# Adding h2 to the node update by an identity product in PSUM instead of an add on VectorE

## The chip, the cores and the metric

One core of a Trainium2 chip runs the whole kernel as one program. The metric is the device time of one execution in microseconds (us). The kernel before took 8569.4 us as the median of three runs (8554.72, 8569.40 and 8579.12).

## What is computed

A stack of four graph layers over 50,000 nodes with 128 features and 25,000 edges: two attention convolutions, three hops of LightGCN, a message-passing layer, and three GCN convolutions. Each layer is entered through a layer norm and relu, and added to its input. The part that the change touches is the third layer's update with what surrounds it:

```
h = max(layernorm(x), 0)                                  # h2
upd = relu([h, aggregated] @ Wu1 + bu1) @ Wu2 + bu2
y = h + upd
out2 = (y - mean(y)) * rsqrt(var(y) + eps) * gamma + beta
x = x + out2                                              # x3
h = max(layernorm(x), 0)                                  # h3
x0 = relu(h @ fc1 + fc1_b); three convolutions; x = x + (... @ fc2 + fc2_b)
```

Most nodes receive no edge, so for them `aggregated` is zero and the convolutions need no neighbours. The kernel computes every node row as if it were such a row, in dense groups, and rows with edges are computed again in later phases that overwrite them.

## The kernel before

The phase `light_and_tail` (`phase_light_and_tail`, class `Tail`) runs two things side by side.

The **tail** does the dense work on all node rows: 98 groups of 4 x 128 rows, each group a tile of 128 partitions x 512 values. It is a software pipeline of 105 steps. In step n, group n is loaded and its first statistics are taken, group n-1 gets h2 and its transpose, group n-2 gets the update and y, group n-3 gets the normed y and x3, group n-4 gets h3 and fc1, and groups n-5 to n-7 go through the convolutions and the output. Every engine has its own function for a step (`vector_step`, `scalar_step`, `tensor_step`, `sync_step`), and inside a step each engine executes its items in the order in which they are written; engines meet only through semaphores. `after(engine, signal, m, k)` makes group m wait until group m-k has given the signal; it is how buffers come free.

The order inside step n that matters here:
- **TensorE**: the update of group n-2 into the PSUM bank `psY` (a bf16 product with ones that brings in the bias bu2, then four products of 128x128 with Wu2); the first convolution of n-5 (`conv_lone`, into `psC1`); the transposes of h2 of n-1 (`psT`); the last convolution of n-6 (`conv2`, into `psU`); the transposes of h3 of n-4; `Wu1a` of n-1; the second convolution of n-5 (`conv1`, into `psC2`); `fc1` of n-4 (`psF`); the output of n-6 (`psO`). A float32 product appears in the trace as two matmuls.
- **ScalarE**: `uT` of n-2 (after Wu1a); `x0T` of n-5 (after fc1 of the step before); h2 of n-1 (four activations on 128x128); `yn` of n-3 (four); a root; `h2T`; `x3T` of n-6 (after conv2); h3 of n-4 (four); two roots; `h3T`.
- **VectorE**: statistics of x of group n; sums of the hops (all but the last of this step); `g2T`; the output add; the addition of beta to x, and the product of `yn` with gamma (both n-3); `g1T` of n-5 (reads `psC1`); x3 of n-3; y of n-2, which is the sum of `psY` and h2 (line 1421); statistics of x3 and of y; the last sum of the step; three pairs of small instructions that turn roots into scale and shift.

There is one bank `psY`. Before the products into it, TensorE waits until the previous group's y has been made (line 1514). `normed` (line 1445) ends with a wait for its own result and then raises the semaphore `scaled`, which says that the statistics' buffers, and the rows it read, are free. The phase uses seven banks for the tail and one for the hops, which are all eight.

The **hops** are the LightGCN sums: 3 x 49 groups, gathered by GpSimd's indirect DMAs and added up on VectorE (lines 1639 and 1648). Of each 35 steps, the first 33 hold one or two such sums, and the last two hold none; in those GpSimd mends the first rows of the table and starts the next hop.

The message phase, later in the program, computes the same update for rows with edges, and there h2 already comes in through an identity product (line 2678), and statistics and `yn` read PSUM (lines 2444 and 2541).

Of the kernel before, what the change touches and what calls it, by code (L numbers as in the profile page):

```python
# [9 lines left out]
ALU = mybir.AluOpType  # L10
# [1107 lines left out]
def after(engine, signal, m, k):  # L1118

    if m >= k:  # L1120
        engine.wait_ge(signal, m - k + 1)
# [186 lines left out]
class Tail:  # L1308
# [6 lines left out]
    def __init__(self, nc, net, out):  # L1315
        self.nc, self.net, self.out = nc, net, out
        sb = lambda n_, shape, dt=F32: nc.alloc_sbuf_tensor(f"tail_{n_}", shape, dt)
        sem = lambda n_: nc.alloc_semaphore(f"tail_{n_}")
        ring = lambda n_, k: sb(n_, [P, k, S, D])
        self.X, self.h2, self.y, self.x3 = ring("x", self.XR), ring("h2", self.HR), ring("y", 3), ring("x3", self.X3R)  # L1320
        self.yn, self.h3, self.h2T, self.uT, self.h3T = (ring(n_, 2) for n_ in ("yn", "h3", "h2T", "uT", "h3T"))
        self.x0T, self.g1T, self.g2T, self.x3T = ring("x0T", 3), ring("g1T", 2), ring("g2T", 2), ring("x3T", 2)
        self.stats, self.mv, self.std, self.nmr = (sb(n_, [P, 3, self.MV, S, k]) for n_, k in (("stats", 6), ("mv", 2), ("std", 1), ("nmr", 1)))
        self.ps = {n_: nc.alloc_psum_tensor(f"tail_ps{n_}", [P, 512], F32) for n_ in ("T", "U", "Y", "F", "C1", "C2", "O")}
        self.x_in = [sem(f"x_in{k}") for k in range(self.XR)]
        self.o_out = [sem(f"o_out{k}") for k in range(self.X3R)]
        self.gathered, self.taken, self.rooted, self.summed, self.inverted, self.scaled = ([sem(f"{n_}{k}") for k in range(3)] for n_ in (
            "gathered", "taken", "rooted", "summed", "inverted", "scaled"))
        self.h2_made, self.h2_turned, self.h2T_made, self.u_done, self.uT_made, self.upd_done, self.y_made, self.yn_made = (sem(n_) for n_ in (
            "h2_made", "h2_turned", "h2T_made", "u_done", "uT_made", "upd_done", "y_made", "yn_made"))  # L1330
        self.xb_made, self.gy_made, self.x3_made, self.h3_made, self.h3_turned, self.h3T_made, self.x0_done, self.x0T_made = (sem(n_) for n_ in (
            "xb_made", "gy_made", "x3_made", "h3_made", "h3_turned", "h3T_made", "x0_done", "x0T_made"))
        self.c1_done, self.g1_made, self.c2_done, self.g2_made, self.c3_done, self.x3T_made, self.o_done, self.o_made = (sem(n_) for n_ in (
            "c1_done", "g1_made", "c2_done", "g2_made", "c3_done", "x3T_made", "o_done", "o_made"))
# [22 lines left out]
    def vector_step(self, v, n, early, late):  # L1357
        nc, w, ps = self.nc, self.net.w, self.ps
        inside = lambda m: 0 <= m < NODE_GROUPS
        stats, mv, std, nmr = self.stats, self.mv, self.std, self.nmr  # L1360

        def statistics(i, m, rows_):
            k = m % self.MV
            after(v, self.scaled[i], m, self.MV)
            for j in range(S):
                last = nc.vector.bn_stats(stats[:, i, k, j, :], rows_[:, j, :])
            last.then_inc(self.gathered[i], 1)
            v.wait_ge(self.gathered[i], m + 1)
            for j in range(S):
                last = nc.vector.bn_aggr(mv[:, i, k, j, :], stats[:, i, k, j, :])  # L1370
            last.then_inc(self.taken[i], 1)

        def invert(i, m):
            if inside(m):
                k = m % self.MV
                v.wait_ge(self.rooted[i], m + 1)
                nc.vector.reciprocal(std[:, i, k, :, 0], std[:, i, k, :, 0]).then_inc(self.summed[i], 1)
                v.wait_ge(self.summed[i], m + 1)
                nc.vector.scalar_tensor_tensor(out=nmr[:, i, k, :, 0], in0=mv[:, i, k, :, 0], scalar=-1.0, in1=std[:, i, k, :, 0],  # L1379
                                               op0=ALU.mult, op1=ALU.mult).then_inc(self.inverted[i], 1)  # L1380
        m = n
        if inside(m):
            v.wait_ge(self.x_in[m % self.XR], 16 * (m // self.XR + 1))
            statistics(0, m, self.X[:, m % self.XR, :, :])
        early()
        m = n - 6
        if inside(m):
            v.wait_ge(self.c2_done, m + 1)
            after(v, self.c3_done, m, 2)
            nc.vector.scalar_tensor_tensor(out=self.rows(self.g2T, 2, m), in0=ps["C2"][:, :], scalar=0.0, in1=self.rows(self.x0T, 3, m),  # L1390
                                           op0=ALU.max, op1=ALU.add).then_inc(self.g2_made, 1)
        m = n - 7
        if inside(m):
            v.wait_ge(self.o_done, m + 1)
            o = self.rows(self.x3, self.X3R, m)
            nc.vector.tensor_tensor(o, ps["O"][:, :], o, ALU.add).then_inc(self.o_made, 1)
        m = n - 3
        if inside(m):
            x2, yn = self.X[:, m % self.XR, :, :], self.yn[:, m % 2, :, :]
            v.wait_ge(self.h2_made, m + 1)  # L1400
            nc.vector.tensor_tensor(x2, x2, slots(w["beta"]), ALU.add).then_inc(self.xb_made, 1)
            v.wait_ge(self.yn_made, m + 1)
            nc.vector.tensor_tensor(yn, yn, slots(w["gamma"]), ALU.mult).then_inc(self.gy_made, 1)
        m = n - 5
        if inside(m):
            v.wait_ge(self.c1_done, m + 1)
            after(v, self.c2_done, m, 2)
            nc.vector.scalar_tensor_tensor(out=self.rows(self.g1T, 2, m), in0=ps["C1"][:, :], scalar=0.0, in1=self.rows(self.x0T, 3, m),
                                           op0=ALU.max, op1=ALU.add).then_inc(self.g1_made, 1)
        m = n - 3  # L1410
        if inside(m):
            v.wait_ge(self.xb_made, m + 1)
            v.wait_ge(self.gy_made, m + 1)
            if m >= self.X3R:
                v.wait_ge(self.o_out[m % self.X3R], 16 * (m // self.X3R))
            nc.vector.tensor_tensor(self.rows(self.x3, self.X3R, m), self.rows(self.yn, 2, m), self.rows(self.X, self.XR, m), ALU.add).then_inc(self.x3_made, 1)
        m = n - 2
        if inside(m):
            v.wait_ge(self.upd_done, m + 1)
            after(v, self.yn_made, m, 3)  # L1420
            nc.vector.tensor_tensor(self.rows(self.y, 3, m), ps["Y"][:, :], self.rows(self.h2, self.HR, m), ALU.add).then_inc(self.y_made, 1)
        m = n - 3
        if inside(m):
            v.wait_ge(self.x3_made, m + 1)
            statistics(2, m, self.x3[:, m % self.X3R, :, :])
        m = n - 2
        if inside(m):
            v.wait_ge(self.y_made, m + 1)
            statistics(1, m, self.y[:, m % 3, :, :])
        late()  # L1430
        invert(0, n)
        invert(2, n - 3)
        invert(1, n - 2)

    def scalar_step(self, act, n):
# [9 lines left out]
        def normed(i, m, out, rows_, func, made):  # L1445
            act.wait_ge(self.inverted[i], m + 1)
            for j in range(S):
                last = nc.scalar.activation(out[:, j, :], rows_[:, j, :], func, bias=self.nmr[:, i, m % self.MV, j, :], scale=self.std[:, i, m % self.MV, j, :])  # L1448
            last.then_inc(made, 1)
            act.wait_ge(made, m + 1)  # L1450
            act.sem_inc(self.scaled[i], 1)
# [9 lines left out]
            nc.scalar.activation(self.rows(self.x0T, 3, m), ps["F"][:, :], ACT.Relu, bias=w["fc1_b"][:, 0:1], scale=1.0 / X0_SCALE).then_inc(self.x0T_made, 1)  # L1461
        m = n - 1
        if inside(m):
            after(act, self.y_made, m, self.HR)
            normed(0, m, self.h2[:, m % self.HR, :, :], self.X[:, m % self.XR, :, :], ACT.Relu, self.h2_made)
        m = n - 3
        if inside(m):
            after(act, self.x3_made, m, 2)
            normed(1, m, self.yn[:, m % 2, :, :], self.y[:, m % 3, :, :], ACT.Identity, self.yn_made)
        root(0, n)  # L1470
        m = n - 1
        if inside(m):
# [20 lines left out]
    def tensor_step(self, pe, n):  # L1493
# [11 lines left out]
        def bias(name, out):  # L1505
            nc.tensor.matmul(ps[out][:, :], net.ones_b[:, :], net.parts[name][:, :, :].rearrange("p j d -> p (j d)"), start=True, stop=False)
# [4 lines left out]
            last.then_inc(done, 1)  # L1511
        m = n - 2
        if inside(m):
            after(pe, self.y_made, m, 1)
            bias("bu2", "Y")
            pe.wait_ge(self.uT_made, m + 1)
            product(self.uT[:, m % 2, :, :], "Wu2", "Y", self.upd_done)
        m = n - 5
# [1481 lines left out]
```

## Time and profile before

| | us |
|---|---|
| median of three runs | 8569.4 |
| the profiled execution, its own time | 8508.76 |
| its span in the trace | 8507.1 |
| the light_and_tail phase in it | about 4009 to 5351 |
| busy over the whole span: PE, VectorE, ScalarE, GpSimd | 3708.8, 4381.7, 2807.7, 3976.6 |

The profiled execution's time is 1.66 us more than its span. Busy times of engines overlap each other. The phase of the change is a sixth of the span, so the shares over the whole span say little about it; rows further down are taken from the phase.

### The profile page before, as it was taken

What the parts mean: (1) busy time and instruction counts of PE and PEld (TensorE: products, weight loads), DVE (VectorE), ACT (ScalarE), POOL (GpSimd) and SP (SyncE); (2) the same over time, 40 slices, a digit from 0 to 9 for tenths busy, and PEclk for the clock granted to TensorE, in tenths of its full rate; (3) what the DMA queues carried; (4) which work ended last, traced back from release to release, by engine and by line L of the source; (5) the groups of instructions that cost most, each with busy time, mean ns of one, the idle gap of its engine ahead of it and who ended that gap; (6) DMA issues with size and microseconds to landing.
All of it is one profiled execution on the core that took longest, in us unless ns stands there. A gap on an engine that the chain in (4) does not pass through costs nothing. (4 is left out here: it accounts for less than half of the span.)

```text
span 8507.1 us, 77896 instructions
## 1 busy us (share of the span) xinstructions
PE 3708.8 (44%) x17298; PEld 2510.9 (30%) x17298; DVE 4381.7 (52%) x16544; ACT 2807.7 (33%) x6612; POOL 3976.6 (47%) x4025
## 2 busy tenths in 40 slices
PE   1501116711133452000676767466657889333333
PEld 1300004401022441000343434344434555223222
DVE  6340007906041741478888979567653445444322
ACT  3800006700031221012566656344433555222111
POOL 0047771062737026334534344466655442566566
PEclk9755558955565666555788889788777778666665
DMA  1000004521033253165334333344332332555433
GB/s 46 3 18 15 17 17 156 191 92 41 15 100 91 78 212 90 27 229 185 95 92 98 98 90 99 120 145 145 136 105 79 99 98 91 182 172 174 132 107 94
DMA packets 463932, 866.81 MB, mean 102 GB/s; under 512 B 110119, under 2 KB 119700, under 8 KB 461932
## 3 DMA queue, kind: packets, MB, share of 16 engines
q1 hardware_dynamic: 349035, 681.67, 23.2%
q0 software_dynamic: 114560, 181.50, 9.5%
q8 instruction: 107, 1.75, 0.1%
q14 instruction: 230, 1.88, 0.1%
HBM read 415.76 MB, written 459.09 MB: 103 GB/s over the span
## 5 line engine op out<-in xcount | busy, mean ns | idle before, releaser
L2756 POOL DMA_INDIRECT gcn_ring<-GT,gcn_index x588 | 590.8, 1005 | 255.0 <-issue 171.3
L1605 POOL DMA_INDIRECT light_ring<-C,light_s_u x392 | 392.2, 1001 | 402.8 <-DVE light_acc L1648 297.5
L1499 PE MATMUL tail_psT<-ident,tail_h 128*128 128x128 f32 x784 | 142.5, 311 | 724.5 <-ACT tail_h L1448 671.5
L2857 DVE SCALAR_TENSOR_TENSOR gcn_acc<-gcn_acc,cont,gcn_ring 128x128 f32<-128x128 f32 x588 | 204.7, 348 | 371.6 <-DMA gcn_ring<-GT,gcn_index 133.8
L532 POOL DMA_INDIRECT got_s<-TAB,src_u x196 | 185.8, 948 | 429.5 <-POOLq L560 366.0
L2366 POOL DMA_INDIRECT msg_ps<-PS,msg_s_u x196 | 189.8, 969 | 354.8 <-PE msg_ps_z L2662 298.1
L1499 PEld LDWEIGHTS tail_psT<-ident,tail_h 128*128 128x128 f32 x784 | 101.2, 155 | 857.3 <-ACT tail_h L1448 750.7
L2939 PE MATMUL gcn_psA<-ident,gcn_h 128*128 128x128 f32 x588 | 132.1, 365 | 498.0 <-DVE gcn_h L2860 253.1
L1448 ACT ACTIVATE tail_h<-tail_x,tail_nmr,tail_std 128x128 f32<-128x128 f32 x784 | 320.6, 483 | 14.4 <-DVE tail_nmr L1379 7.3
L2906 ACT ACTIVATE gcn_hT<-gcn_psA 128x512 f32<-128x512 f32 x147 | 88.6, 603 | 638.4 <-DMA X3D<-msg_x 245.9
L539 POOL DMA_INDIRECT J<-sort_items,sort_place x196 | 191.1, 975 | 199.1 <-POOLq L1714 137.0
L1605 POOL DMA_INDIRECT light_ring<-HD,light_r_u x196 | 195.1, 996 | 180.7 <-DVE light_acc L1648 127.8
L1024 POOL DMA_INDIRECT out<-source_rows_o,source_out_places x208 | 216.3, 1040 | 96.5 <-issue 57.3
L2749 POOL DMA_INDIRECT out<-gcn_x_then_o,own_idx_u x196 | 208.9, 1066 | 106.2 <-issue 62.9
L1297 PE MATMUL front_a_psS<-w_W,front_a_h1T 128*128 128x136 f32 x640 | 108.3, 318 | 337.6 <-issue 190.7
L1008 POOL DMA_INDIRECT source_rows_xs<-XHX,xs_places x208 | 211.8, 1018 | 93.4 <-issue 65.0
L1217 DVE RECIPROCAL front_a_std<-front_a_std 128x4 f32<-128x4 f32 x80 | 12.1, 152 | 449.8 <-issue 260.1
L2939 PEld LDWEIGHTS gcn_psA<-ident,gcn_h 128*128 128x128 f32 x588 | 87.8, 183 | 526.2 <-DVE gcn_h L2860 266.9
L958 PE MATMUL gcn_psB<-w_conv,gcn_hT 128*128 128x128 f32 x784 | 143.5, 342 | 227.6 <-issue 119.2
L532 POOL DMA_INDIRECT got_d<-TAB,dst_u x196 | 206.2, 1052 | 66.5 <-issue 66.5
L539 POOL DMA_INDIRECT J<-packed,sort_place x196 | 195.9, 1000 | 76.8 <-issue 70.7
L435 POOL DMA_INDIRECT gat_ring<-T,gat_stage x196 | 194.2, 991 | 68.7 <-issue 66.2
(615 smaller groups left out, 14266.2 us busy)
## 6 DMA issues: line engine op xcount, KB each, us to landing
T<-front_a_t SPq DMA_DIRECT2D x160, 272.0 KB
source_rows_c<-C SPq DMA_DIRECT2D x156, 256.0 KB
GT<-source_rows_r SPq DMA_DIRECT2D x156, 256.0 KB
C<-light_acc SPq DMA_DIRECT2D x147, 256.0 KB
gcn_own<-GT SPq DMA_DIRECT2D x147, 256.0 KB
RC<-gcn_own SPq DMA_DIRECT2D x147, 256.0 KB
gat_rows_r<-RG SPq DMA_DIRECT2D x104, 264.0 KB
RG<-gat_rows SPq DMA_DIRECT2D x2, 12936.0 KB
```

Of the source, the lines that this page charges most:

```text
L435: nc.gpsimd.indirect_dma_start(out=ring[:, half, u, :], out_offset=None, in_=table, in_offset=bass.IndirectOffsetOnAxis(ap=stage[:, half, ...
L532: nc.gpsimd.indirect_dma_start(out=out[:, c, :], out_offset=None, in_=table, in_offset=bass.IndirectOffsetOnAxis(ap=index[:, c:c + 1], axi ...
L539: nc.gpsimd.indirect_dma_start(out=table, out_offset=bass.IndirectOffsetOnAxis(ap=index[:, c:c + 1], axis=0), in_=rows[:, c, :], in_offset ...
L1008: nc.gpsimd.indirect_dma_start(out=rows[g][:, j, :], out_offset=None, in_=table, in_offset=bass.IndirectOffsetOnAxis(ap=b["places"][:, g, ...
L1024: nc.gpsimd.indirect_dma_start(out=out, out_offset=bass.IndirectOffsetOnAxis(ap=b["places"][:, g, j:j + 1], axis=0), in_=rows[g][:, j, :], ...
L1448: last = nc.scalar.activation(out[:, j, :], rows_[:, j, :], func, bias=self.nmr[:, i, m % self.MV, j, :], scale=self.std[:, i, m % self.MV ...
L1499: last = nc.tensor.transpose(ps["T"][:, j * P:(j + 1) * P], rows_[:, j, :], net.ident[:, :])
L1605: nc.gpsimd.indirect_dma_start(out=ring[:, n % RING, j, :], out_offset=None, in_=tables[h], in_offset=bass.IndirectOffsetOnAxis(ap=index[: ...
L2749: nc.gpsimd.indirect_dma_start(out=out, out_offset=bass.IndirectOffsetOnAxis(ap=net.own_idx_u[:, m * S + j:m * S + j + 1], axis=0), in_=o[ ...
L2756: nc.gpsimd.indirect_dma_start(out=ring[:, n % RING, j, :], out_offset=None, in_=net.GT[i], in_offset=bass.IndirectOffsetOnAxis(ap=index[: ...
L2857: nc.vector.scalar_tensor_tensor(out=acc[:, n % 2, j, :], in0=before, scalar=net.cont[:, c:c + 1], in1=ring[:, n % RING, j, :], op0=ALU.mu ...
L2939: ins = nc.tensor.transpose(psA[n % 2][:, j * P:(j + 1) * P], h[:, n % 2, j, :], net.ident[:, :])
```

## The change

The buffer `y` and the semaphore `y_made` go. Line numbers are those of the kernel before.

```diff
@@ vector_step
         m = n - 2
         if inside(m):
             v.wait_ge(self.upd_done, m + 1)
-            after(v, self.yn_made, m, 3)
-            nc.vector.tensor_tensor(self.rows(self.y, 3, m), ps["Y"][:, :], self.rows(self.h2, self.HR, m), ALU.add).then_inc(self.y_made, 1)
+            statistics(1, m, ps["Y"][:, :].rearrange("p (j d) -> p j d", j=S))
         m = n - 3
         if inside(m):
             v.wait_ge(self.x3_made, m + 1)
             statistics(2, m, self.x3[:, m % self.X3R, :, :])
-        m = n - 2
-        if inside(m):
-            v.wait_ge(self.y_made, m + 1)
-            statistics(1, m, self.y[:, m % 3, :, :])
@@ scalar_step
         m = n - 1
         if inside(m):
-            after(act, self.y_made, m, self.HR)
+            after(act, self.upd_done, m, self.HR)
             normed(0, m, self.h2[:, m % self.HR, :, :], self.X[:, m % self.XR, :, :], ACT.Relu, self.h2_made)
         m = n - 3
         if inside(m):
             after(act, self.x3_made, m, 2)
-            normed(1, m, self.yn[:, m % 2, :, :], self.y[:, m % 3, :, :], ACT.Identity, self.yn_made)
+            normed(1, m, self.yn[:, m % 2, :, :], ps["Y"][:, :].rearrange("p (j d) -> p j d", j=S), ACT.Identity, self.yn_made)
@@ tensor_step
         m = n - 2
         if inside(m):
-            after(pe, self.y_made, m, 1)
+            after(pe, self.scaled[1], m, 1)
             bias("bu2", "Y")
+            nc.tensor.matmul(ps["Y"][:, :], net.ident[:, :], self.rows(self.h2, self.HR, m), start=False, stop=False)
             pe.wait_ge(self.uT_made, m + 1)
             product(self.uT[:, m % 2, :, :], "Wu2", "Y", self.upd_done)
```

## Rows read from the trace of the kernel before

**Rows 1.** Window: us; busy (count) of PE, PEld, DVE, ACT, POOL; granted clock; DMA share; GB/s.

```profile
4009.00:5351.00 1342.00, 901.51 (x3534) 514.34 (x3534) 1123.35 (x4353) 830.58 (x1959) 586.38 (x588) 0.85 0.36 95
```

**Rows 2.** Timeline of VectorE, the adds at line 1421: start us, duration us, instruction.

```profile
4490.70 0.68 DVE L1421 TENSOR_TENSOR tail_y<-tail_psY,tail_h 128x512 f32<-128x512 f32 x1
...
4913.71 0.69 DVE L1421 TENSOR_TENSOR tail_y<-tail_psY,tail_h 128x512 f32<-128x512 f32 x1
...
4955.03 0.68 DVE L1421 TENSOR_TENSOR tail_y<-tail_psY,tail_h 128x512 f32<-128x512 f32 x1
```

**Rows 3.** Timeline of TensorE, one step.

```profile
4722.35 0.38 PE L1506 MATMUL tail_psY<-parts_bu,ones_b 128*128 128x512 bf16 x1
4722.57 1.05 PE L1510 MATMUL tail_psY<-w_Wu,tail_uT 128*128 128x128 f32 x8
4723.46 1.02 PE L1503 MATMUL tail_psC<-tail_x0T,w_conv_lone 128*128 128x512 f32 x2
4724.32 0.60 PE L1499 MATMUL tail_psT<-ident,tail_h 128*128 128x128 f32 x4
4724.76 1.02 PE L1503 MATMUL tail_psU<-tail_g2T,w_conv 128*128 128x512 f32 x2
4728.45 1.12 PE L1499 MATMUL tail_psT<-ident,tail_h 128*128 128x128 f32 x4 [2.67 <-ACT tail_h L1448]
4729.36 1.92 PE L1503 MATMUL tail_psU<-tail_h2T,w_Wu1a 128*128 128x512 f32 x2
4731.07 1.14 PE L1503 MATMUL tail_psC<-tail_g1T,w_conv 128*128 128x512 f32 x2
4732.04 1.02 PE L1503 MATMUL tail_psF<-tail_h3T,w_fc 128*128 128x512 f32 x2
...
4733.12 1.05 PE L1510 MATMUL tail_psO<-w_fc,tail_x3T 128*128 128x128 f32 x8
```

**Rows 4.** Timeline of ScalarE, the same step and the start of the next.

```profile
4723.84 1.65 ACT L1448 ACTIVATE tail_yn<-tail_y,tail_nmr,tail_std 128x128 f32<-128x128 f32 x4 [0.17 <-ACT tail_h L1448]
...
4726.28 0.59 ACT L1480 ACTIVATE tail_x3T<-tail_psU 128x512 f32<-128x512 f32 x1
4726.76 1.64 ACT L1448 ACTIVATE tail_h<-tail_x,tail_nmr,tail_std 128x128 f32<-128x128 f32 x4
...
4733.10 0.69 ACT L1461 ACTIVATE tail_x0T<-tail_psF,w_fc_b 128x512 f32<-128x512 f32 x1 [1.10 <-PE tail_psF L1503]
4733.69 1.63 ACT L1448 ACTIVATE tail_h<-tail_x,tail_nmr,tail_std 128x128 f32<-128x128 f32 x4
```

**Rows 5.** Timeline of VectorE, the same step and the start of the next.

```profile
4726.13 0.68 DVE L1408 SCALAR_TENSOR_TENSOR tail_g1T<-tail_psC,tail_x0T 128x512 f32<-128x512 f32 x1
...
4733.27 0.87 DVE L1366 BATCH_NORM_STATS2 tail_stats<-tail_x 128x6 f32<-128x128 f32 x4
```

**Rows 6.** Groups by line and form in the phase: count, busy us, mean ns, idle before.

```profile
L1421 DVE TENSOR_TENSOR tail_y<-tail_psY,tail_h 128x512 f32<-128x512 f32 x98 | 67.0, 683 | 0.0
L1366 DVE BATCH_NORM_STATS2 tail_stats<-tail_y 128x6 f32<-128x128 f32 x392 | 82.6, 275 | 0.6 <-issue 0.4
L1448 ACT ACTIVATE tail_yn<-tail_y,tail_nmr,tail_std 128x128 f32<-128x128 f32 x392 | 161.4, 482 | 18.6 <-issue 10.2 <-ACT tail_h L1448 6.4 <-DMA XHX<-front_b_x 1.9
```

**Rows 7.** Groups by line and form in the message phase, both reading PSUM.

```profile
L2444 DVE BATCH_NORM_STATS2 msg_stats<-msg_ps_upd 128x6 f32<-128x128 f32 x197 | 42.5, 279 | 11.1 <-PE msg_ps_upd L2681 11.0
...
L2541 ACT ACTIVATE msg_yn<-msg_ps_upd,msg_nmr,msg_std 128x128 f32<-128x128 f32 x197 | 74.1, 456 | 28.3 <-DVE msg_nmr L2459 27.3 <-issue 0.9
```

**Rows 8.** Timeline of TensorE in the message phase, an identity product.

```profile
6617.08 1.91 PE L2678 MATMUL msg_ps_upd<-msg_h,ident 128*128 128x512 f32 x2
```

**Rows 9.** Timeline of TensorE in the tail, after a shorter idle stretch.

```profile
4439.64 0.66 PE L1499 MATMUL tail_psT<-ident,tail_h 128*128 128x128 f32 x4 [2.45 <-ACT tail_h L1448]
4440.13 1.02 PE L1503 MATMUL tail_psU<-tail_h2T,w_Wu1a 128*128 128x512 f32 x2
4440.99 1.02 PE L1503 MATMUL tail_psC<-tail_g1T,w_conv 128*128 128x512 f32 x2
```

More of the change, by code:

```diff
@@ L1319, in __init__ @@
         ring = lambda n_, k: sb(n_, [P, k, S, D])
-        self.X, self.h2, self.y, self.x3 = ring("x", self.XR), ring("h2", self.HR), ring("y", 3), ring("x3", self.X3R)
+        self.X, self.h2, self.x3 = ring("x", self.XR), ring("h2", self.HR), ring("x3", self.X3R)
         self.yn, self.h3, self.h2T, self.uT, self.h3T = (ring(n_, 2) for n_ in ("yn", "h3", "h2T", "uT", "h3T"))
@@ L1328, in __init__ @@
             "gathered", "taken", "rooted", "summed", "inverted", "scaled"))
-        self.h2_made, self.h2_turned, self.h2T_made, self.u_done, self.uT_made, self.upd_done, self.y_made, self.yn_made = (sem(n_) for n_ in (
-            "h2_made", "h2_turned", "h2T_made", "u_done", "uT_made", "upd_done", "y_made", "yn_made"))
+        self.h2_made, self.h2_turned, self.h2T_made, self.u_done, self.uT_made, self.upd_done, self.yn_made = (sem(n_) for n_ in (
+            "h2_made", "h2_turned", "h2T_made", "u_done", "uT_made", "upd_done", "yn_made"))
         self.xb_made, self.gy_made, self.x3_made, self.h3_made, self.h3_turned, self.h3T_made, self.x0_done, self.x0T_made = (sem(n_) for n_ in (
```

## The prediction

> **What bounds the kernel now.** I read the windows view of the phase first. Over its 1342 us VectorE is busy 1123 us, TensorE 902 and ScalarE 831 [rows 1], so VectorE looks like the bound, and an instruction taken off it looks like a gain. The second view is the timeline of the adds that go: between two interruptions at the hops' ends they run from 4490.70 to 4913.71 in 34 steps, a mean of 12.44 us a step; the interval across a hop's end is 41.3 us [rows 2]. Of the 97 intervals four are long (two hop ends, two at the phase's start, where loads are late), and 93 are of the 12.44 kind. Third, the timelines of TensorE, ScalarE and VectorE over one step, laid side by side [rows 3 to 5], because the change alters who waits for whom. There the reader is to see that TensorE begins the update (its first item of a step) at 4722.35, while ScalarE finishes `yn`, its fourth item of the same step, only at 4723.84 + 1.65 = 4725.49, 3.1 us later [rows 3, 4]. By then TensorE has also done the first convolution and nearly the transposes of h2. Before the change nothing ties the two: y left `psY` in the step before.
>
> **What is removed.** 98 adds on VectorE. The mean of one is 683 ns, but starts overlap, and one costs the engine about 0.60 us; 67.0 us of busy time in all, at most 98 x 0.60 = 59 us of path [rows 6]. The statistics read PSUM in place of the buffer y: 279 ns against 275 in the message phase [rows 6, 7], under 0.02 us for four, taken as nothing.
>
> **What ScalarE gains.** `yn` read from PSUM has a mean of 456 ns against 482 from the buffer; by busy time over count it is 74.1/197 = 0.376 against 161.4/392 = 0.412 us [rows 6, 7]. Four make 0.14 us a step.
>
> **What TensorE gains in work.** One identity product of 128x512 in float32, two matmuls. The convolution of the same shape runs from 4723.46 until the transposes start at 4724.32, that is 0.86 us at full clock [rows 3]; the message phase's identity product took 1.91 for its two matmuls with the drain, about twice the 1.02 that the convolution takes [rows 3, 8]. So 0.86 to 1.71 us a step; I take 0.86, and treat the clock below.
>
> **What moves: the wait.** The only bank `psY` is now held until `yn` of that group has been made. Since `scaled` of group n-3 is raised by ScalarE in step n, and the update of group n-2 is TensorE's first item in step n, everything TensorE does in a step is now queued behind `yn` of that step. `yn` in turn stands behind x0T, and that behind fc1 of TensorE's step before. So a closed loop arises through both in-order engines, and its length is the shortest a step can be. I walk it once round with the rows, from the end of one `yn` to the end of the next:
>
> 1. ScalarE's wait for its own result, 0.17 as between its groups [rows 4], and about 0.13 for the handover and the bias product's weights (an estimate: a handover alone is 0.04 to 0.05 in items 3 and 5, and the weights come on top): 0.30.
> 2. TensorE, bias 4722.35 to the end of conv2 at 4724.76 + 1.02 = 4725.78 is 3.43 [rows 3]; with the identity product 4.29.
> 3. Handover 0.04, x3T 0.48 until the h3 activations start, these 1.64, handover 4728.45 - 4728.40 = 0.05 [rows 3, 4]: 2.21.
> 4. TensorE, transposes of h3, Wu1a, conv1, fc1: 4728.45 to 4732.04 + 1.02 = 4733.06 is 4.61 in this step [rows 3]. Where the clock held it is 0.49 and 0.86 from starts [rows 9], 0.86 more for conv1, and 1.02: 3.23.
> 5. Handover 0.04, x0T 0.59 until h2's activations start, these 1.63, 0.17, `yn` 1.65 less the 0.14: 3.94 [rows 4].
>
> The sum is 0.30 + 4.29 + 2.21 + 3.23 + 3.94 = 13.97 us at full clock throughout.
>
> **The clock.** Matmuls take either the full-clock time or twice it: in rows 3 the two Wu1a matmuls need 1.92 us after an idle stretch of 2.67, where after 2.45 they needed 1.02 [rows 9]; the mean granted clock of the phase is 0.85 [rows 1]. In the other steps that I read, too, the burst behind TensorE's long idle stretch ran partly at 1.2 GHz, and partly at 2.4; in rows 3 that cost 4.61 - 3.23 = 1.4 us, elsewhere up to 1.7. The loop splits TensorE's one idle stretch into two. Before h3's transposes it is 2.2 us (item 3), which mostly was short enough. Before the update it is the time from the output product's end to `yn`'s: fc1 ends, ScalarE needs 3.94, and TensorE meanwhile works about 1.1 (4733.12 + 1.05 - 4733.06), so with the 0.3 of item 1 about 3.1 us idle. I therefore expect one drop a step, priced at 1.6: 13.97 + 1.6 = 15.57 us.
>
> What else is late? VectorE after `yn`: gamma, then `g1T` must wait for the first convolution, which now comes 0.3 + 0.22 + 0.86 + 0.89 + 1.02 = 3.3 us after `yn`, and 4.9 with the drop. From `g1T` to the next step's statistics VectorE needs 7.14 less the add's 0.60, so 6.54 [rows 5], and the scale and shift that h2's activations want are made before that: at 3.3 + 6.54 = 9.8, or 11.5 with the drop, while those activations start 3.9 - 0.6 = 3.3 before the next `yn` ends, at 12.3. So it comes in time. Its whole round is a mean of 12.44 less 0.60 = 11.84 us even if it never idled [rows 2, 6], and a loop of 15.57 leaves it 3.7 us free, which will stand ahead of gamma and `g1T`. Gathers of the hops run ahead in eight buffers, and only get more time. The freed 0.60 us of VectorE is worth nothing.
>
> **The sum.** 15.57 - 12.44 = 3.13 us a step; over 93 steps 291 us. The two intervals at hop ends contain the same loop plus a standstill of all engines: 3.1 each, 6 us. The two at the start wait for loads: nothing (at most 6). That makes +297 us. The profiled execution's own time is 8508.8, so it would be 8806; it ran 60.6 us below the median shown, and what is timed is compared with the median, so the forecast is 8569.4 + 297 = 8866 us.
>
> The Trainium skill (Perfetto Trace Analysis, Matmuls) says independent matmul groups should rotate through different PSUM banks so that the evacuation of one overlaps the next group's matmuls. It speaks against this change in the same direction as the loop. Its Matmul Optimizations section adds that all eight banks should be in use; here they are, one per purpose, and no ninth is there for `psY`. It names no price; the sum stands on the rows alone.
>
> **Rivals.**
> - **No drop of the clock** (chance 0.12): two shorter idle stretches in place of a long one, as in rows 9. For it speaks that the transposes' gap shrinks; against, the 3.1 us before the update. Then 13.97 - 12.44 = 1.53, times 95 is 145: 8715 us.
> - **A drop in both bursts** (0.27): the mean clock of the phase would fall to about 0.8. For it: a burst of 4.3 us is shorter than the one of some 12 us before, so less work stands ahead of the 2.2 us idle stretch. Step 13.97 + 3.2 = 17.17; 4.73 x 95 = 449: 9019 us.
> - **VectorE remains the bound and the loop closes under it: faster** (0.02). The mechanism: ScalarE runs ahead of TensorE, `yn` is done when TensorE comes to the update, and the step shrinks by the add's 0.60: 59 us less, 8510. It decides at the point where `yn` ends no later than TensorE's arrival; in rows 3 and 4 it ends 3.1 us after. ScalarE can't run ahead, since x0T waits 1.10 us for fc1 [rows 4], so I give it almost nothing. The Trainium skill (Perfetto Trace Analysis, Optimizing Scalar/DVE Operations) gives VectorE about 60 ns of access on SBUF and 125 on PSUM: four statistics would lose 0.26 us, and this rival's gain would be 0.34 a step, 33 us. Rows 6 and 7 don't bear that out (275 and 279 ns).
> - **No difference** (0.02): a wait of TensorE that its 2.67 us idle stretch later in the step absorbs. That would hold if the stretch were slack; but the stretch waits for h3, which stands behind conv2, which is pushed out by the wait itself.
>
> **How the numbers follow.** One drop has 0.57, with its own range of 8800 to 8930 (a step 0.7 us off either way). The range at 8 in 10 takes it and nearly all of the case with two: 8740 to 9020. Faster and slower mean by more than 0.3%, 26 us, about what can be told from no change: faster 0.02, the same 0.02, slower 0.96.
>
> **What would show it.** In the trace after: the distance from one `yn` to the next 15 to 16 us, with and without an early sum alike; the bias product starting about 0.3 us after `yn`'s end, with the longest idle of TensorE now before it, released by ScalarE; VectorE idle 2 to 4 us before `g1T`; VectorE's busy share of the phase down from 0.84 to about 0.65; `yn` near 456 ns. I am wrong if the bias product starts before `yn` ends, if VectorE is still busy nine tenths of each step, or if steps with two sums are longer than those with one.

## The result, and the profile after

The changed kernel takes 8972.0 us (median of four runs, 8952.8 to 8986.5) against 8574.3 for the kernel before (four runs, the three shown ahead and the one taken beside the changed kernel). The ratio is 1.0456, 95% interval 1.0412 to 1.0500: slower by 391 us by the ratio, 398 by the medians. The forecast was 8866, its range 8740 to 9020, and its chance for slower 0.96.

The changed kernel's profiled execution took 8986.5 us, its span is 8984.8. From the first statistics of the tail to the last scatter of the hops, the phase took 5350.8 - 4002.6 = 1348 us before and 5778.5 - 4015.3 = 1763 after: 415 more. The other phases, whose code is the same, differ by the remaining 63 us between these two single executions. In a second pair of profiled executions, both on one chip (r_before and r_changed below), the spans are 417.6 us apart and the phase 409.9, so the added time lies in the phase.

The windows view of the phase after, in the columns of [rows 1]:

```profile
4013.00:5778.00 1765.00, 1167.99 (x3680) 679.25 (x3730) 1081.16 (x4265) 834.90 (x1960) 592.46 (x596) 0.79 0.28 73
```

VectorE is busy for 0.61 of it (0.84 before), so it no longer bounds the phase. TensorE's granted clock has gone from 0.85 to 0.79 of full. The timeline of TensorE over one step (start, duration, instruction, and in brackets the idle time ahead of it) answers to [rows 3]:

```profile
4718.12 0.39 PE L1501 MATMUL tail_psY<-parts_bu,ones_b 128*128 128x512 bf16 x1 [2.93 <-ACTq L1446]
4718.35 1.02 PE L1511 MATMUL tail_psY<-tail_h,ident 128*128 128x512 f32 x2
4719.21 1.76 PE L1505 MATMUL tail_psY<-w_Wu,tail_uT 128*128 128x128 f32 x8
4720.76 1.91 PE L1498 MATMUL tail_psC<-tail_x0T,w_conv_lone 128*128 128x512 f32 x2
4722.47 0.76 PE L1494 MATMUL tail_psT<-ident,tail_h 128*128 128x128 f32 x4
4723.06 1.02 PE L1498 MATMUL tail_psU<-tail_g2T,w_conv 128*128 128x512 f32 x2
4726.31 1.12 PE L1494 MATMUL tail_psT<-ident,tail_h 128*128 128x128 f32 x4 [2.22 <-ACT tail_h L1443]
4727.22 1.92 PE L1498 MATMUL tail_psU<-tail_h2T,w_Wu1a 128*128 128x512 f32 x2
4728.93 1.37 PE L1498 MATMUL tail_psC<-tail_g1T,w_conv 128*128 128x512 f32 x2
4730.13 1.02 PE L1498 MATMUL tail_psF<-tail_h3T,w_fc 128*128 128x512 f32 x2
```

and the timeline of ScalarE over the same step and into the next to [rows 4]:

```profile
4716.52 1.50 ACT L1443 ACTIVATE tail_yn<-tail_psY,tail_nmr,tail_std 128x128 f32<-128x128 f32 x4 [0.17 <-issue]
...
4724.12 0.60 ACT L1475 ACTIVATE tail_x3T<-tail_psU 128x512 f32<-128x512 f32 x1 [0.26 <-PE tail_psU L1498]
4724.62 1.64 ACT L1443 ACTIVATE tail_h<-tail_x,tail_nmr,tail_std 128x128 f32<-128x128 f32 x4
...
4731.19 0.69 ACT L1456 ACTIVATE tail_x0T<-tail_psF,w_fc_b 128x512 f32<-128x512 f32 x1 [1.33 <-PE tail_psF L1498]
4731.78 1.64 ACT L1443 ACTIVATE tail_h<-tail_x,tail_nmr,tail_std 128x128 f32<-128x128 f32 x4
4733.59 1.51 ACT L1443 ACTIVATE tail_yn<-tail_psY,tail_nmr,tail_std 128x128 f32<-128x128 f32 x4 [0.17 <-issue]
```

The reader is to see the loop in them. `yn` ends at 4718.02; the bias product of the update starts 0.10 later, and its 2.93 us of idle end on ScalarE's queue at line 1446 of the changed kernel, which is where `normed` waits for its own result and raises `scaled`. From `yn`'s end to the next one's, 4735.10, are 17.08 us. VectorE stands still in the middle, ahead of `g1T` (its timeline in the same step, against [rows 5]):

```profile
4718.06 0.69 DVE L1403 TENSOR_TENSOR tail_yn<-tail_yn,w_gamma 128x512 f32<-128x512 f32 x1 [1.53 <-ACT tail_yn L1443]
4722.71 0.69 DVE L1408 SCALAR_TENSOR_TENSOR tail_g1T<-tail_psC,tail_x0T 128x512 f32<-128x512 f32 x1 [3.96 <-PE tail_psC L1498]
```

Read from the products with gamma, one a step, the 33 undisturbed intervals between the first and the second hop end are all 17.06 to 17.08 us, with one sum or two alike; the mean of all 97 is 17.46 against 13.23 before, which makes 411 us.

### The profile page after: what moved, and what is told of

Read it like the earlier page. It is cut to its first block and busy times, and to the rows that moved or that the text cites. A ratio compares the mean times of both kernels' runs of the same rounds, so it can differ in the third digit from the quotient of the medians.

```text
span 8984.8 us, 77930 instructions
## 1 busy us (share of the span) xinstructions
PE 3982.7 (44%) x17329; PEld 2692.3 (30%) x17494; DVE 4316.0 (48%) x16446; ACT 2811.8 (31%) x6612; POOL 3988.8 (44%) x4025
## 5 line engine op out<-in xcount | busy, mean ns | idle before, releaser
L1494 PE MATMUL tail_psT<-ident,tail_h 128*128 128x128 f32 x784 | 181.3, 375 | 621.7 <-issue 386.9
L1494 PEld LDWEIGHTS tail_psT<-ident,tail_h 128*128 128x128 f32 x784 | 140.8, 205 | 807.9 <-issue 494.0
L1024 POOL DMA_INDIRECT out<-source_rows_o,source_out_places x208 | 234.5, 1127 | 96.5 <-issue 63.6
L1408 DVE SCALAR_TENSOR_TENSOR tail_g1T<-tail_psC,tail_x0T 128x512 f32<-128x512 f32 x98 | 67.7, 691 | 368.0 <-PE tail_psC L1498 268.9
```

The costliest lines, as they stand in the source:

```text
L1024: nc.gpsimd.indirect_dma_start(out=out, out_offset=bass.IndirectOffsetOnAxis(ap=b["places"][:, g, j:j + 1], axis=0), in_=rows[g][:, j, :], ...
L1494: last = nc.tensor.transpose(ps["T"][:, j * P:(j + 1) * P], rows_[:, j, :], net.ident[:, :])
```

## The experiments

The runs of this section fell on three chips, each group with its own runs of the kernel before: 8616 us for e1 to e4, 7252 us for e5 to e8, 8511 us for the last four. Ratios are each to the kernel before on the same chip; the second chip is compared by ratio or by step length only. Step lengths are those of single profiles.

**The wait alone.** In the kernel before:

```diff
-            after(pe, self.y_made, m, 1)
+            after(pe, self.scaled[1], m, 1)
```

> The kernel before with one line changed: TensorE waits for `scaled` of the previous group ahead of the update, in place of the signal that y was made. No identity product, VectorE still adds h2, y stays in SBUF. If the wait is what closes the loop (my theory), a step is the changed kernel's 17.07 us less the identity product's 0.86, plus the 0.14 that `yn` loses when it reads SBUF again: 16.35 us, the same in every step, and 93 x (16.35 - 12.44) = 364 us more than the kernel before, 8920 to 8940 us. If TensorE's added work is what costs (rival one), or the reading of PSUM by VectorE and ScalarE (rival two), this run takes what the kernel before takes, 8574 within 30 us.

8850.4 us, ratio 1.0272 (1.0249 to 1.0295): 235 us slower, by one wait and not one instruction more. Both rivals are out as the whole cause, and my number for it was too high. The steps aren't equal: between the hop ends they take 13.07, about 14.5, 16.2 to 16.5 or 17.6 us. TensorE's timeline shows two of them in a row:

```profile
4716.05 0.39 PE L1506 MATMUL tail_psY<-parts_bu,ones_b 128*128 128x512 bf16 x1 [3.07 <-ACTq L1451]
4716.28 1.05 PE L1510 MATMUL tail_psY<-w_Wu,tail_uT 128*128 128x128 f32 x8
4717.17 1.02 PE L1503 MATMUL tail_psC<-tail_x0T,w_conv_lone 128*128 128x512 f32 x2
...
4730.32 0.39 PE L1506 MATMUL tail_psY<-parts_bu,ones_b 128*128 128x512 bf16 x1 [3.07 <-issue]
4730.55 1.05 PE L1510 MATMUL tail_psY<-w_Wu,tail_uT 128*128 128x128 f32 x8
4731.44 1.77 PE L1503 MATMUL tail_psC<-tail_x0T,w_conv_lone 128*128 128x512 f32 x2
```

Behind the same 3.07 us of idle the convolution runs at full clock once and mostly at 1.2 GHz the next time. 13.07 is the walked loop at full clock, without the identity product: 0.10 + 3.43 + 2.23 + 3.23 + 4.08. So here drops come in some bursts, not in both of every step, as I had assumed. By the clock records of the traces, 102 of e1's 192 bursts that follow TensorE's wait for `scaled` or for h3 ran in part at 1.2 GHz, and 190 of the changed kernel's 192. The wait alone is thus 235 of the 391 us. What is left for the rest is the identity product on the loop, an estimated 0.72 us a step (0.86 less the 0.14 that `yn` gains), and the drops that now come in nearly every burst; no run parts these two.

**The product alone.** In the kernel before, the identity product added, and at the add's place:

```diff
-            nc.vector.tensor_tensor(self.rows(self.y, 3, m), ps["Y"][:, :], self.rows(self.h2, self.HR, m), ALU.add).then_inc(self.y_made, 1)
+            nc.vector.tensor_copy(self.rows(self.y, 3, m), ps["Y"][:, :]).then_inc(self.y_made, 1)
```

> The kernel before with the identity product of h2 in PSUM, but VectorE copies PSUM into y at the place of the add, so y, its signal and the early release of the bank stay. My theory: TensorE has an idle stretch of 2.7 us in each step that takes up 0.86 us of work, VectorE has a copy for an add of the same length, so 8574 us within 30. Rival one, the work costs: 98 x 0.86 = 84 us at full clock, up to 168 at half, so 8660 to 8740 us.

8619.0 us, ratio 1.0006 (0.9989 to 1.0022). With the loop open, 98 identity products cost at most 19 us. VectorE's copy is no shorter than its add (683 ns by the median of 98), so the run is a fair one:

```profile
L1421 DVE COPY tail_y<-tail_psY x98: 676/683/691, 4059.1 to 5379.4; 128x512 f32<-128x512 f32 x98
```

**Two banks.** In the changed kernel:

```diff
-            after(pe, self.scaled[1], m, 1)
+            after(pe, self.scaled[1], m, 2)      # and psY0, psY1 in turn for psY
```

> The changed kernel with two banks for the update, used in turn, so that TensorE waits for `yn` of the group before the last, which ScalarE made a step earlier. The bank comes from the hops' carry, whose three products of 128x128 and their waits are left out (VectorE adds a tile of zeros in their place). My theory: the loop is open, VectorE is the bound again and has 0.60 us less to do a step: 8574 - 59 = 8515 us, between 8490 and 8560, and TensorE has its clock back. If work or PSUM reads are what costs, the time stays above 8850 us.

8619.1 us, ratio 1.0007 (0.9993 to 1.0022). The loop is open and nearly all of the 391 us are gone; the 59 us that I expected on top aren't there. Steps with two sums take 12.3 us, 0.6 less than before, as VectorE's missing add makes them. But steps with one sum, which took 11.0 to 14.4, now mostly take 12 to 15. My reading, which this run doesn't test, is that the older loop through both engines (fc1, output, update, conv, transposes, conv2, h3, Wu1a, conv1, fc1), which doesn't pass `yn`, holds the update, and that the identity product makes it longer. Added up at full clock from [rows 3, 4, 9], with the output taken as long as the update, it is 9.8 us before, 10.7 with the product, 12.3 with one drop. What lies above 12.3 is in waits of ScalarE ahead of `h2T` that the profile puts down to nothing it knows ("remote"):

```profile
L1470 ACT ACTIVATE tail_h2T<-tail_psT 128x512 f32<-128x512 f32 x98 | 58.5, 597 | 171.8 <-remote 136.5 <-issue 23.8 <-PE tail_psT L1494 8.9
```

I didn't find their cause.

**The update later in TensorE's step.** In the changed kernel the whole block, wait, bias, identity product and product, stands behind conv2:

```diff
@@ tensor_step: the block of m = n - 2, first in the step
-        m = n - 2
-        if inside(m):
-            after(pe, self.scaled[1], m, 1)
-            ...
@@ ahead of m = n - 4, h3's transposes
+        m = n - 2
+        if inside(m):
+            after(pe, self.scaled[1], m, 1)
+            ...
```

> The changed kernel, still one bank, with the update moved in TensorE's order from the first item of a step to behind the last convolution of n-6, ahead of the transposes of h3. By my theory `yn` is then done, or nearly so, when TensorE gets there: the update ends about 2.4 us after `yn`, and TensorE has until 3.0 us after it, when h3 is ready. The loop shrinks to under 12 us and VectorE bounds again. VectorE takes the statistics of y ahead of those of x3 and may wait up to 0.6 us for them, so between 8515 and 8575 us. If the clock drops in the update as before, 1.6 us more a step in those steps where TensorE is late, 8600 to 8700. If the work is what costs, above 8850 us.

8550.2 us, ratio 0.9921 (0.9895 to 0.9946): with the identity product, with PSUM reads, with one bank held until `yn` is done, it is faster than the kernel before. In us it was to be 8515 to 8575 beside 8574; this chip's kernel before takes 8616, the ratio makes 8506 of 8574, just under that. The second run of the same kernel, on the third chip, gave 0.9966 (0.9949 to 0.9982). TensorE's timeline around `yn`'s end at 4716.88, and VectorE's statistics of y:

```profile
4715.74 1.02 PE L1498 MATMUL tail_psU<-tail_g2T,w_conv 128*128 128x512 f32 x2
4716.97 0.39 PE L1501 MATMUL tail_psY<-parts_bu,ones_b 128*128 128x512 bf16 x1 [0.21 <-issue]
4717.20 1.02 PE L1527 MATMUL tail_psY<-tail_h,ident 128*128 128x512 f32 x2
4718.06 1.05 PE L1505 MATMUL tail_psY<-w_Wu,tail_uT 128*128 128x128 f32 x8
4719.84 0.66 PE L1494 MATMUL tail_psT<-ident,tail_h 128*128 128x128 f32 x4 [0.73 <-ACT tail_h L1443]
```

```profile
4719.15 0.89 DVE L1366 BATCH_NORM_STATS2 tail_stats<-tail_psY 128x6 f32<-128x128 f32 x4 [0.29 <-PE tail_psY L1505]
```

The wait is still there and costs TensorE 0.21 us in this step; the update then lies where TensorE had stood idle for h3.

**And the order on VectorE.** On top of the run before, the statistics of y go behind those of x3 again:

```diff
@@ vector_step
-            v.wait_ge(self.upd_done, m + 1)
-            statistics(1, m, ps["Y"][:, :].rearrange("p (j d) -> p j d", j=S))
         m = n - 3
         if inside(m):
             v.wait_ge(self.x3_made, m + 1)
             statistics(2, m, self.x3[:, m % self.X3R, :, :])
+        m = n - 2
+        if inside(m):
+            v.wait_ge(self.upd_done, m + 1)
+            statistics(1, m, ps["Y"][:, :].rearrange("p (j d) -> p j d", j=S))
```

> The run with the update later on TensorE, and VectorE taking the statistics of y behind those of x3 again, as in the kernel before, instead of ahead of them. In e4_update_later VectorE stood 0.1 to 0.3 us ahead of the statistics of y, and the mean step was 12.09 us. If that wait is what keeps VectorE from the full 0.60 us, a step is 11.9 us, 93 x 0.2 = 19 us less than e4_update_later: ratio to the kernel before 0.988 to 0.991. If the step hangs on something else, the ratio stays 0.992 or comes out above it, since `yn`'s scale is then made later.

7209.0 us, ratio 0.9941 (0.9928 to 0.9955) on the second chip; on the third, beside e4's kernel, 0.9936 (0.9914 to 0.9959) against 0.9966. Both lie above the 0.988 to 0.991 that I expected. Steps with two sums went from 12.74 to 12.42 us there, which is VectorE's wait gone; but of the steps with one sum many went from 10.70 to about 11.6, so the mean of all 97 fell only from 12.81 to 12.70. Why the short steps got longer isn't shown. The intervals of the two ratios overlap, so that it is better than the run before is likely, not settled.

**The place alone.** In the kernel before, its update block (with the wait for `y_made`) moved in the same way, with nothing of the change:

> The kernel before with nothing of the change, but with the update moved behind the last convolution in TensorE's order. It tells the gain of e4_update_later apart into the place and the missing add. In the kernel before the closed path of both in-order engines (fc1, x0T, h2, conv2, h3, fc1) holds the update, 1.1 us; moved into the idle stretch it leaves the path, and steps with one sum fall to VectorE's 11.0 us. If the place is what gained: a step of 12.2 us, ratio 0.995 to 0.998, and e4_update_later's missing add is worth only the rest. If the missing add is what gained: 1.000 within 0.002. A third outcome, the add on VectorE waiting for the later update by over 0.5 us, would be above 1.003.

7245.1 us, ratio 0.9989 (0.9980 to 0.9999). The place alone gains 0.1%, less than the 0.2 to 0.5% of my first guess; so of e5's 0.6% on the same chip 0.5%, some 36 us, come with the change itself, the add gone and the product in. This is the part of the change's purpose that was really to be had, once the wait is harmless. A higher clock alone isn't what gains: TensorE's granted clock between hop ends is 0.89 in the kernel before and 0.97 in e4 (4530 to 4910), but on the second chip it is 0.94 in e6, which gains almost nothing, and 0.96 in e5 (3700 to 4100).

**TensorE kept busy.** In the changed kernel, ahead of the wait for `scaled` and of the wait for h3:

```diff
+        fill(14)          # at the start of the step
...
+        fill(11)          # ahead of h3's transposes
+    for _ in range(k):
+        nc.tensor.matmul(ps[:, D:4 * D], net.ones_b[:, :], net.parts["bu2"][:, 0:3, :].rearrange("p j d -> p (j d)"), start=True, stop=True)
```

> The changed kernel with TensorE's idle stretches filled: ahead of its wait for `scaled` 14 products of 128x384 in bf16 (2.2 us at full clock), and ahead of its wait for h3 11 of them (1.8 us), into the unused columns of the hops' bank; results unused. Not in the steps around a hop's end. It tells the clock's share from the wait's. My theory, two clock drops of 1.6 us in each step: they go, a step is 13.97 us, the walked loop at full clock, so 93 x (17.07 - 13.97) = 288 us less than the changed kernel: ratio to the kernel before about 1.012 to 1.016. Rival, the bursts are slow for another reason than what TensorE did before them (the order of banks, the loads): a step stays at 17 us or gets longer, ratio 1.045 or more.

7427.5 us, ratio 1.0247 (1.0231 to 1.0262). Timelines of TensorE and of ScalarE:

```profile
3803.46 2.44 PE L1685 MATMUL light_ps<-parts_bu,ones_b 128*128 128x384 bf16 x14
3806.55 0.39 PE L1502 MATMUL tail_psY<-parts_bu,ones_b 128*128 128x512 bf16 x1 [0.65 <-ACTq L1446]
3806.77 1.02 PE L1512 MATMUL tail_psY<-tail_h,ident 128*128 128x512 f32 x2
3807.63 1.05 PE L1506 MATMUL tail_psY<-w_Wu,tail_uT 128*128 128x128 f32 x8
3808.52 1.02 PE L1499 MATMUL tail_psC<-tail_x0T,w_conv_lone 128*128 128x512 f32 x2
```

```profile
3804.95 1.50 ACT L1443 ACTIVATE tail_yn<-tail_psY,tail_nmr,tail_std 128x128 f32<-128x128 f32 x4 [0.17 <-ACT tail_h L1443]
...
3818.73 1.50 ACT L1443 ACTIVATE tail_yn<-tail_psY,tail_nmr,tail_std 128x128 f32<-128x128 f32 x4 [0.17 <-ACT tail_h L1443]
```

In the filled steps the bursts are at full clock (the granted clock from 3300 to 4634 is 0.99), and `yn` comes every 13.78 us: the walked loop of 13.97, with the handover of 0.10 in place of the 0.30 I had put (13.77). Against the 17.07 of the changed kernel on the other chips, 3.3 us of a step are clock; against the 12.44 of the kernel before there, 1.3 are the longer path. The ratio that I expected was too low because I took it from the first chip's times. On this chip hop ends cost no standstill, and the mean of all 97 intervals is 11.87 us in e6, which is within about 0.1% of the kernel before; in e7 it is 13.80. 97 x 1.93 = 187 us is about what was measured, 176. The changed kernel itself wasn't run on this chip.

**`yn` first on ScalarE.** In the changed kernel:

```diff
@@ scalar_step: the block of m = n - 3, which stood third, now first
+            normed(1, m, self.yn[:, m % 2, :, :], ps["Y"][:, :].rearrange("p (j d) -> p j d", j=S), ACT.Identity, self.yn_made)
         m = n - 2
         if inside(m):
             act.wait_ge(self.u_done, m + 1)
```

> The changed kernel with one bank, TensorE's order kept, and `yn` moved to the front of ScalarE's step, ahead of uT, x0T and h2. If the loop runs through fc1, x0T and h2's activations to `yn`, as I say, it opens: `yn` is made in ScalarE's idle time before x0T, and TensorE finds the bank free. Then it behaves as with two banks (e3_two_banks), ratio to the kernel before 0.997 to 1.006. Rival, holding the bank until any `yn` is itself the cost, wherever it stands: ratio above 1.02.

7244.5 us, ratio 0.9991 (0.9982 to 1.0000). TensorE's timeline, the update of two steps in a row:

```profile
3808.65 0.38 PE L1501 MATMUL tail_psY<-parts_bu,ones_b 128*128 128x512 bf16 x1
...
3820.03 0.39 PE L1501 MATMUL tail_psY<-parts_bu,ones_b 128*128 128x512 bf16 x1 [0.47 <-ACTq L1446]
```

The bank is one, the wait is on TensorE's first item, the product is in: only the path from fc1 to `yn` is cut, and the loss is gone, though TensorE still waits 0.47 us for the bank in every other step. That names the mechanism most closely.

**Both kernels again, and both versions with a later update, on one chip.**

> The kernel before once more, for its profile on the chip of this group. The two groups of runs so far fell on chips whose times for the kernel before differ by 16% (8616 and 7252 us), and on the second chip loads and hop ends cost almost no standstill. If the added time is a closed loop of engine work, as I say, steps are the same there: 12.9 us with two sums, 11.0 with one, mean 11.9 to 12.5.

> The changed kernel once more, beside the others of its group. By my theory its step doesn't hang on the chip's DMA speed: 17.07 us each. Then it takes 95 x (17.07 - 11.9 to 12.4) = 440 to 490 us more than the kernel before on a chip like the second, less what hop ends absorb, ratio 1.055 to 1.065 there, and 1.042 to 1.050 on a chip like the first. If the added time came from memory traffic, the ratio would shrink on the faster chip.

> The changed kernel with the update behind conv2 on TensorE (e4_update_later) again, on the same chip as the next one, to rank the two. Ratio 0.991 to 0.995.

> The same with VectorE's statistics of y behind those of x3 (e5_later_both) again. By my theory VectorE's wait of 0.1 to 0.3 us ahead of the statistics goes: 0 to 0.2% below r_later. If the two are level within 0.1%, the order on VectorE is worth nothing.

8498.3 us (one run); 8916.2 us, ratio 1.0482 (1.0450 to 1.0514); and the two ratios given above. The kernel before takes 12.87 us for steps with two sums here, as on the first chip. The changed kernel's step is 17.07 us on this chip too, but for a few steps at the phase's start and behind each hop end, which take 11.3 to 16.5. This chip is like the first one, with standstills at the hop ends, so it doesn't test what the changed kernel would do on the second.

## Why the prediction was right

**Direction and mechanism: shown.** The loop from `yn` through TensorE and back is in the trace, e1 makes it with one wait, and three different cuts (another bank, another place on TensorE, another place on ScalarE) each remove the loss. The bias product starts behind `yn`, VectorE falls to 0.61 (I had said 0.65), `g1T` waits 3.96 us (2 to 4 were named), and steps with one sum and with two are equal. The distance from one `yn` to the next was to be 15 to 16 us and is 17.07.

**The loop's items.** Of 13.97 us at full clock, measured 13.78; the handover was 0.10 and not 0.30. With the drops, the changed kernel's items are 0.10, 5.96 (4.29), 2.23 (2.21), 4.84 (3.23) and 3.95 (3.94), the walked ones in brackets: 17.08. ScalarE's and the handovers' items are right to 0.02.

**The clock: the term that was mis-sized.** I expected one drop a step at 1.6 us, and gave two drops 0.27. There are two, in nearly every step, of 1.67 and 1.61 us in the step shown. What failed is the premise that the 2.2 us of idle ahead of h3's transposes "mostly was short enough". It rested on one burst that kept its clock behind 2.45 us [rows 9]. The same trace says the opposite of 2.22 us: h3's transposes follow an idle stretch of that length 22 times in the kernel before, and by the clock records each of these bursts ran for 2.9 to 3.4 us at 1.2 GHz. In 20 of the 22 a further idle stretch, of 1.45 to 1.82 us, lay only about 1.1 us of work earlier. The burst just ahead of that of rows 9 is one of them:

```profile
4424.54 1.13 PE L1503 MATMUL tail_psU<-tail_g2T,w_conv 128*128 128x512 f32 x2 [1.46 <-DVE tail_g2T L1390]
4427.88 1.11 PE L1499 MATMUL tail_psT<-ident,tail_h 128*128 128x128 f32 x4 [2.22 <-ACT tail_h L1448]
4428.79 1.91 PE L1503 MATMUL tail_psU<-tail_h2T,w_Wu1a 128*128 128x512 f32 x2
```

Two readings beside it were off as well: the bursts of the kernel before that begin with h3's transposes mostly last 7.4 to 10.4 us and not some 12, and the one ahead of rows 9 was itself at 1.2 GHz for its first 3 us. It is tempting to lay the drops on the short work between two idle stretches. As a whole rule that doesn't hold: e1 has stretches of 3.07 and 2.22 us with less work between them than the changed kernel, and 90 of its 192 bursts kept the full clock. What decides in the single case stays open. The likeliest time was thus the wrong one of my two, 106 us below the result, and that the result lies in the range is due to the second case having been counted into it; the rival with two drops gave 9019.

**Hop ends.** I charged them the full gain of a step each. They took less: the three intervals around a hop end make 10.97 + 22.02 + 31.60 = 64.6 us before, and 17.07 + 40.66 + 10.52 = 68.3 after, so 3.7 more and not three times 4.6. With two hop ends that is 20 us less than the rival's 449, and 17.07 in place of 17.17 us a step another 9; the 97 intervals together came to 411, so some 9 us lie in smaller things. The medians, 398 apart, aren't those of the two profiled executions.

**The small terms.** The statistics from PSUM have a mean of 284 ns against 275, and `yn` from PSUM 457 against 482 [rows 6], as the message phase's rows said [rows 7]. The groups by line in the phase after:

```profile
L1366 DVE BATCH_NORM_STATS2 tail_stats<-tail_psY 128x6 f32<-128x128 f32 x392 | 86.7, 284 | 19.6 <-remote 18.0 <-PE tail_psY L1505 1.6
L1443 ACT ACTIVATE tail_yn<-tail_psY,tail_nmr,tail_std 128x128 f32<-128x128 f32 x392 | 147.5, 457 | 16.8 <-issue 8.5 <-ACT tail_h L1443 8.1
```

By busy time over count `yn` gained 0.412 - 0.376 = 0.036 us, to the third digit what was forecast.

**What I said of the freed add** held for the changed kernel: worth nothing behind the loop. It didn't say that the change is worth 36 us of the add's possible 59 once the update is placed elsewhere.

## What to carry to other kernels

When an instruction's last reader changes, look where that reader stands in its engine's order, and walk round from it: if the writer is the first item of its engine's step, everything behind it inherits the wait. A closed walk over two in-order engines, with durations from one step of the trace, gave the step at full clock to 0.2 us before anything was run (13.97 against 13.78). The changed kernel's own step, 17.07, was 1.5 us longer than the forecast 15.57: a second drop, less the 0.2 of the handover. Moving the waiting block to where its engine already stands idle cost nothing, and turned 4.6% slower into 0.3 to 0.8% faster. And price TensorE's idle time twice, as waiting and as clock. For the second price count what the trace at hand shows behind idle stretches of the length in question, all of them and not one: 22 of 22 here. Even that is a chance and not a rule, as e1's 52 of 86 behind the same 2.22 us show.

## What the hardware showed that I had not expected

In the changed kernel, idle stretches of 2.93 and 2.22 us, with about six us of work between them, brought TensorE to 1.2 GHz for a part of 190 of 192 bursts: 3.3 of the step's 17.07 us. The same 3.07 us of idle in e1 was followed by full clock in one step and by half in the next, and 2.22 us by half in all 22 cases of the kernel before, but in e1 in only 52 of 86. So the length of the last idle stretch alone doesn't tell which clock a burst gets.

The kernel before took 8616, 7252 and 8511 us on three chips, while the tail's steps with two sums took 12.88 us in the profiles of the kernel before and, with VectorE's same work, in e6 on the second chip. Around both hop ends e6 shows no standstill on that chip. So it isn't the engines' speed in the tail that differs. Of the 1246 us between the spans of r_before and e6, 726 lie ahead of the phase and 136 in it. Why, no run here tells.
